# Contextual attention, two layers of four images on one core: feature buffers twice, sums ahead of arguments, exponentials behind copies

## What is computed

```python
raw_w = patches(b, 4, 2)                    # L = 1600 patches of 64 x 4 x 4
f = b[:, :, ::2, ::2]                       # 40 x 40
w = patches(f, 3, 1)                        # 1600 patches of 64 x 3 x 3
wn = w / maximum(norm(w), 1e-4)
yi = einsum('bpd,bld->blp', w, wn) * mm     # scores, 1600 x 1600
yi = softmax(yi * 10, axis=1) * mm
patches = einsum('blp,bld->bpd', yi, raw_w)
out = overlap_add(patches, stride 2)[pad:-pad] / 4
```

## Time and profile before

| | before |
|---|---|
| median of 3 runs | 1486.64 us (1485.1 to 1486.96) |
| the profiled execution, its own time | 1485.93 us |
| its span, first to last instruction | 1484.1 us |
| TensorE matmul, weight load busy | 1340.5 us (90%), 904.1 us (61%) |
| VectorE, ScalarE busy | 1195.3 us (81%), 853.7 us (58%) |
| GpSimd busy | 47.6 us |
| mean granted TensorE clock | 0.973 |

### The profile page before, as it was taken

One profiled execution on the slowest core, in us unless ns is written; L12 is line 12 of the kernel. 1 busy time (PEld: TensorE's weight loads), 2 busy tenths in 40 slices (PEclk: granted clock), 3 DMA queues, 4 the chain that ended last, 5 costly groups with the idle time before them and its releaser, 6 DMA issues.

```text
span 1484.1 us, 24228 instructions
## 1 busy us (share of the span) xinstructions
PE 1340.5 (90%) x7190; PEld 904.1 (61%) x7190; DVE 1195.3 (81%) x2830; ACT 853.7 (58%) x2233; POOL 47.6 (3%) x63
## 2 busy tenths in 40 slices
PE   4987999989999799998999899998999989999796
PEld 4765755667556675576656576566755666557343
DVE  4667889779888798878897878977888879888883
ACT  2667646656457564585555754666655755458431
POOL 1000000010000100001000000000000010000100
PEclk9997999999999999999999999999999999999999
DMA  5305462155622744137631556215462255412442
GB/s 101 45 1 133 108 130 70 51 150 116 127 61 65 172 101 109 52 85 165 122 93 34 130 128 136 78 44 143 119 124 72 62 143 113 111 51 83 129 137 57
DMA packets 181749, 146.57 MB, mean 99 GB/s; under 512 B 120114, under 2 KB 177522, under 8 KB 181618
## 3 DMA queue, kind: packets, MB, share of 16 engines
q1 hardware_dynamic: 181298, 144.04, 41.0%
q10 hardware_dynamic: 320, 0.99, 0.3%
HBM read 19.76 MB, written 13.11 MB: 22 GB/s over the span
## 4 chain that ended last, share of the span: by engine, by line
PE 32%; DVE 28%; SPq 11%; ACT 11%; issue 10%; DMA 7%; DVEq 0%; POOL 0%; ACTq 0%; POOLq 0%
PE psG L465 14%; PE psO L515 14%; DVE G L934 7%; DVE Z L967 5%; DVE G L874 4%; SPq L318 4%; DVE S L880 4%; DVE G L945 4%; ACT S L690 3%; ACT G L701 3%; SPq L299 3%; DMA HV<-LOHI 3%; PE psG L474 3%; ACT G L676 3%; DMA SH<-G 3%
## 5 line engine op out<-in xcount | busy, mean ns | idle before, releaser
L515 PE MATMUL psO<-Z,B 123*128 123x492 f32 (+2 forms) x1792 | 718.4, 530 | 38.5 <-DVE Z L967 25.2
L515 PEld LDWEIGHTS psO<-Z,B 123*128 123x128 f32 x1792 | 326.4, 194 | 238.1 <-issue 129.9
L465 PE MATMUL psG<-LH,HL 128*123 128x246 f16 (+2 forms) x2616 | 411.8, 287 | 38.2 <-DMA HV<-LOHI 28.7
L465 PEld LDWEIGHTS psG<-LH,HL 128*123 128x123 f16 x2616 | 280.5, 139 | 161.0 <-issue 96.7
L880 DVE CUSTOM_DVE_ANT_0 S<-G,RB 123x492 f32<-123x492 f32 (+1 forms) x448 | 269.1, 607 | 87.4 <-DVE G L874 55.0
L701 ACT ACTIVATE G<-G,nb 123x492 f32<-123x492 f32 (+1 forms) x448 | 267.0, 642 | 110.9 <-DVE G L934 110.4
L690 ACT ACTIVATE S<-S,nm 123x480 f32<-123x480 f32 (+3 forms) x560 | 307.3, 555 | 2.3 <-DVE nm L885 2.1
L945 DVE TENSOR_TENSOR G<-G,SH 123x492 f32<-123x492 f32 (+1 forms) x448 | 247.3, 591 | 54.2 <-DMA SH<-G 53.9
L934 DVE SCALAR_TENSOR_TENSOR G<-G,RA,psB 123x492 f32<-123x492 f32 (+1 forms) x448 | 270.1, 646 | 0.5 <-issue 0.5
L676 ACT ACTIVATE G<-psG 123x492 f32<-123x492 f32 (+3 forms) x256 | 120.1, 472 | 173.0 <-PE psG L465 92.5
L967 DVE TENSOR_TENSOR Z<-G 123x984 f32<-123x984 f32 (+2 forms) x192 | 197.3, 1028 | 0.6 <-PE psO L515 0.6
(11 more groups left out here) (83 smaller groups left out, 581.3 us busy)
## 6 DMA issues: line engine op xcount, KB each, us to landing
SH<-G SPq DMA_DIRECT2D x336, 214.8 KB
SH<-G SPq DMA_DIRECT2D x112, 89.2 KB
SH<-G SPq DMA_DIRECT2D x336, 19.2 KB
XP<-x SPq DMA_DIRECT2D x20, 280.0 KB, 5.9
XP<-mid SPq DMA_DIRECT2D x20, 280.0 KB, 5.3
HL<-LOHI SPq DMA_DIRECT2D x16, 246.5 KB, 3.5
mid<-OSB SPq DMA_DIRECT2D x48, 80.0 KB, 2.3
out<-OSB SPq DMA_DIRECT2D x48, 80.0 KB, 2.3
```

Source lines behind the costliest of these rows:

```text
L465: last = pe.matmul(psG[0:TW, bank, b0 * TW:b1 * TW], st[:, p:p + TW], mv[:, lo:lo + n], start=i == 0, stop=i == len(terms) - 1)
L515: last = pe.matmul(psO[:, b, 0:n], B[:, o:o + 128], Z[:, 2 * (s % 2) + j, 0:n], start=t == 0, stop=t == TILES - 1)
```

## The change

- `HL`, `LH`, `H1` and `HV` have two buffers each, taken in turn by the unit. ScalarE and VectorE write the high and low parts straight into the two halves of `LH`, so `LOHI` and the two DMAs for `LH` are gone: six DMAs (`N_F`) instead of eight.
- SyncE issues them in slots 10, 11 and 12 (one tile, two DMAs, each), behind the shifts and the strip of the slot, for unit w, instead of all in slot 28. They wait for the products of unit w - 2.
- VectorE: shifted sums and Z come first in every slot. The two arguments of the slot (now `argument_tile`) stand inside the score pair, after the add of the even tile and before its maximum; in slots without scores after Z; in slot 24 at the end, as before. `lse_sum` of slot 29 moves behind Z.
- The first Z of a chunk: its second half, which needs no strip, is made first, and only then comes the wait for the strip.
- ScalarE: the exponentials of the arguments stand behind both copies; in slot 24 the logarithm stands before the odd copy.
- TensorE: in slot 24 the row of logarithms is spread after the block group instead of before.
- Four memsets of the feature tiles and one of `LOHI` become one of `LH`.

```diff
-        HL = sb("HL", [128, FLEN], F16)   (and LH, H1, HV)
+        LH = sb("LH", [128, 2, FLEN], F16)   (and HL, H1, HV)
-        LOHI = sb("LOHI", [128, FLEN], F16)
-        LS, HS = LOHI[0:64, :], LOHI[64:128, :]
...
+        def halves_of(w):
+            return LH[0:64, w % 2, :], LH[64:128, w % 2, :]
...
             def lay_out_features(w, which):
+                if w >= 2:
+                    sp.wait_ge(g_ready, (w - 1) * NB)
+                    sp.sem_inc(sp_gate, 1)
...
-                    if s == SLOTS and w is not None:
-                        sp.wait_ge(g_ready, (v + 1) * NB)
-                        sp.sem_inc(sp_gate, 1)
-                        lay_out_features(w, ("HL", "LH", "H1", "HV"))
                     at = place(u, v, s + LEAD)
                     if at:
                         shift_pair(at)
                     at = place(u, v, s + 2)
                     if at and at[2] == 0:
                         shift_strip(at)
+                    if s in (10, 11, 12) and w is not None:
+                        lay_out_features(w, (("HL", "H1", "HV")[s - 10],))
...
-                    if s == 24 and v is not None:
-                        lse_row(v, w, 0)
...
                     if v is not None and 21 <= s < SLOTS - 1:
                         block_group(v, w, s - 21)
+                    if s == 24 and v is not None:
+                        lse_row(v, w, 0)
...
-            def high_features(v, w):
+            def high_features(w):
                 act.wait_ge(feat_in, (w + 1) * STRIPS * 16)
-                if v is not None:
+                if w >= 2:
                     act.sem_inc(act_gate, 1)
-                    act.wait_ge(f_in, (v + 1) * N_F * 16)
+                    act.wait_ge(g_ready, (w - 1) * NB)
...
                         copy_scores(u, v, j, 0)
+                        if s == 24:
+                            lse_log(v, False)
+                        copy_scores(u, v, j, 1)
                         if at and n == 0 and s != 24:
                             softmax_pair(at)
-                        copy_scores(u, v, j, 1)
                         if s == 23:
                             lse_exp(v, False)
-                        if s == 24:
-                            lse_log(v, False)
...
                         dve.tensor_tensor((odd if par else even)[:, b0 * TW:n], rows[:, p0 * TW:p0 * TW + n - b0 * TW],
                                           psG[0:TW, par, b0 * TW:n], ALU.add).then_inc(read, 1)
+                    if at and par == 0:
+                        argument_tile(at, 0)
+                        argument_tile(at, 1)
                     dve.wait_ge(s_read, v * NB + 2 * j + par + 1)
...
-                if i == 0:
-                    dve.wait_ge(shj_in, (u * NK + k + 1) * 16 * len(STRIP_PARTS))
-                    dve.sem_inc(dve_gate, 1)
...
-                    dve.tensor_tensor(Z[:, slot, 0:n], g[:, 0, c0:c0 + n], SHJ[:, 0:n], ALU.add)
-                    dve.tensor_tensor(Z[:, slot + 1, 0:n], g[:, 1, c0:c0 + n], g[:, 0, c0 - TW:c0 - TW + n],
-                                      ALU.add).then_inc(z_made, 1)
+                    dve.tensor_tensor(Z[:, slot + 1, 0:n], g[:, 1, c0:c0 + n], g[:, 0, c0 - TW:c0 - TW + n], ALU.add)
+                    dve.wait_ge(shj_in, (u * NK + k + 1) * 16 * len(STRIP_PARTS))
+                    dve.tensor_tensor(Z[:, slot, 0:n], g[:, 0, c0:c0 + n], SHJ[:, 0:n], ALU.add).then_inc(z_made, 1)
...
             def body(u, v, w):
                 for s in BODY:
                     at = place(u, v, s + LEAD)
-                    if at and s != 24:
-                        if s == SLOTS + 1:
-                            lse_sum(v, True)
-                        argument_pair(at)
                     at_y = place(u, v, s + AHEAD)
                     if at_y:
                         add_shifted(at_y)
...
                     if s == SLOTS + 1 and v is not None:
+                        lse_sum(v, True)
+                    pairs = score_list(s) if v is not None else []
+                    if at and not pairs:
+                        argument_tile(at, 0)
+                        argument_tile(at, 1)
+                    if s == SLOTS + 1 and v is not None:
                         lse_columns(v, True)
-                    if v is not None:
-                        for j in score_list(s):
-                            score_pair(v, j)
+                    for n, j in enumerate(pairs):
+                        score_pair(v, j, at if n == 0 and s != 24 else None)
...
-            pool.memset(LOHI[:, :].bitcast(F32), 0.0).then_inc(cleared, 1)
```

More of the change, by code:

```diff
@@ L244, in out_parts, with packs @@
                         yield a, j, at[0] - first, len(at), rows[at[0]] - 1 + a
-        def packs(which):
+        def halves_of(w):
+            return LH[0:64, w % 2, :], LH[64:128, w % 2, :]
+        def packs(w, which):
             n = FLEN
-            parts = {"HL": ((HL[0:64, :], HS), (HL[64:128, :], LS)), "LH": ((LH[0:64, :], LS), (LH[64:128, :], HS)),
-                     "H1": ((H1[0:64, :], HS), (H1[64:128, 0:n - 1], HS[:, 1:n])),
-                     "HV": ((HV[0:64, :], HS), (HV[64:128, 0:n - TW], HS[:, TW:n]))}
+            low, high = halves_of(w)
+            hl, h1, hv = (a[:, w % 2, :] for a in (HL, H1, HV))
+            parts = {"HL": ((hl[0:64, :], high), (hl[64:128, :], low)),
+                     "H1": ((h1[0:64, :], high), (h1[64:128, 0:n - 1], high[:, 1:n])),
+                     "HV": ((hv[0:64, :], high), (hv[64:128, 0:n - TW], high[:, TW:n]))}
             return [part for name in which for part in parts[name]]
@@ L297, in lay_out_features @@
                 sp.wait_ge(l_made, 2 * (w + 1))
-                for dst, src in packs(which):
+                for dst, src in packs(w, which):
                     sp.dma_start(dst, src).then_inc(f_in, 16)
@@ L457, in one_row, with products @@
                 return [(HL, LH, dy, dx) for dx in range(3)] + [(H1, H1, dy, 0), (HL, HL, dy, 2)]
-            def products(j, par, bank, b0, b1, terms):
+            def products(v, j, par, bank, b0, b1, terms):
                 s0 = S_CHUNKS[j // PAIRS][0]
@@ L488, in even_tile @@
                 if shared:
-                    last = products(j, 0, 0, stored, w, one_row(0))
+                    last = products(v, j, 0, 0, stored, w, one_row(0))
                 last.then_inc(g_ready, 1)
@@ L497, in odd_tile @@
                 if alone > stored:
-                    products(j, 1, 1, stored, alone, TERMS)
+                    products(v, j, 1, 1, stored, alone, TERMS)
                 if alone < w:
-                    last = products(j, 1, 1, alone, w, one_row(2))
+                    last = products(v, j, 1, 1, alone, w, one_row(2))
                 last.then_inc(g_ready, 1)
@@ L783, in _ @@
             act.wait_ge(l_made, 2)
-            for dst, src in packs(("LH", "HV")):
+            for dst, src in packs(0, ("HV",)):
                 act.dma_start(dst, src).then_inc(f_in, 16)
@@ L924, in lse_columns, with argument_tile @@
                 dve.tensor_tensor(lse[:, t], tot[:, t], big[:, t], ALU.max).then_inc(lse_dve, 1)
[L926 removed]
+            def argument_tile(at, j):
                 u, k, i = at
                 c0, n = p_cols(k)
[L929 removed]
+                t = arg_tiles(i)[j]
+                if i == 0 and j == 0:
                     dve.wait_ge(lse_rows, u * NK + k + 1)
                     dve.sem_inc(dve_gate, 1)
[L932 to L936 removed]
+                g = G[:, t * GLEN + c0:t * GLEN + c0 + n]
+                dve.scalar_tensor_tensor(out=g, in0=g, scalar=RA[:, bass.ds(u * TILES + t, 1)],
+                                         in1=psB[0:TW, k % 2, 0:n],
+                                         op0=ALU.mult, op1=ALU.subtract).then_inc(arg_made, 1)
             def add_shifted(at):
```

37 lines of the change are left out of this document (16 added, 21 removed).

## The result

The changed kernel takes 1552.96 us (median of 4 runs, 1551.22 to 1554.74) against 1486.8 us of the kernel before on the same chip: ratio 1.0446, 95% interval 1.0427 to 1.0464. Slower was forecast, but by 15 us and not by 66, and the time lies outside the range.

What follows compares the result with a forecast made beforehand. TensorE was taken as the limit in chunks 1 and 2, level with VectorE in chunk 0. 1485.9 + 11 (seven bodies) + 7 (last body) - 2 (ends) = 1502 us; range 1460 to 1522, the forecast's own 1489.5 to 1515.

Steps and rivals of the forecast that it cites:

- Features twice: At the boundary, TensorE's products no longer wait for feature copies: 3.1 to 5.0 us at each of 7, 22 to 35 us.
- Anchors (a) and (b): (a) slot 7's paste waits for ScalarE's read-out, moving 0.4 us; (b) slot 9's shift behind SyncE's stores and loads, 0.3 us.
- Strips: Z would wait for late strips: 2.2 us in slot 6, 1.5 in slot 13, 3.5 in slot 20, 1.8 in slot 27.
- In the bodies with scores this still fits: Arguments, exponentials and shift DMAs come 2.3 to 2.9 us later in the slot, but the shifts have two slots.
- rival 4: Shift DMAs become the bound in scored bodies too, when issue and landing exceed 5.5 us in chunk 0: 1558 us; chance 0.10.
- Bubble between add and maximum: VectorE's 0.19 us gap in the even tile is filled where VectorE sets the pace, chunk 0: 1 us per body.
- Copies at the new place: SyncE issues 5.4 us more in slots 10 to 12; it fits, cost 0 to 0.6 us per body, taken as 0.
- Where it gains again: Slots 21 to 27: sooner Z, logarithm ahead of the odd copy, row behind the block group give 1.5 us net per body.
- Last body: Without scores, the chain from sum to sum makes 3.95 us per slot instead of 3.53; with the strips, +7 us.
- TensorE busy 164 us within 1 per body: A sign: TensorE's busy time per body stays 164 us within 1, since the products' count and shapes are the same.
- Rival 2: TensorE makes its lags up, so only the boundary counts: 1469 us, or 1456 at 5.0 us per boundary; chance 0.07.
- Ends: First body gains 1.5 us in slots 24 to 28; the start saves 0.5 us from two small copies and three memsets.

Runs made afterwards that it cites:

- features kernel: Against the kernel before: only the feature buffers twice and six copies in slots 10 to 12, every order as before; 1446.72 us, ratio 0.9734.
- experiment 4: Against the changed kernel: arguments back ahead of both sums and exponentials back between the two copies; 1434.8 us, ratio 0.9656.
- experiment 10: Against the changed kernel: each tile shifted by one transfer of 122 partitions instead of two of 112 and 10; 2471.19 us, ratio 1.6612.

## Why the prediction was wrong

The step that failed is the delay of arguments, exponentials and shifts, taken as a fixed 2.3 to 2.9 us that "in the bodies with scores" still fits. With it the forecast came to +1.6 us a body and +7 us in the last one. Measured were +7.5 us a body (mean of six, 177.1 to 184.6) and +22.5 us at the end, and the arguments' place behind the two sums alone costs 134.4 us between otherwise equal kernels.

Sum of the medians, from before: 1486.7 - 40.0 (features) - 11.9 (small orders) + 48.4 (arguments behind the adds) + 86.1 (behind Z) - 14.6 (exponentials behind the copies) - 1.7 (arguments behind the even add) = 1553.0. Each term is a difference of neighbouring kernels above, in this order; in another order they would differ, since the moves interact (the exponentials' move alone is +26 on early arguments).

- **Features twice: right in kind, at the upper edge.** 22 to 35 us gross were forecast for seven boundaries. In the traces of before and of the features kernel the seven boundaries give 34.1 us of VectorE's time, 4.2 at the example and 4.8 to 5.2 at the others; the medians differ by 40.0. VectorE follows TensorE further than the 3.1 us of the lower edge. The example boundary had the shortest wait for the copies, 2.27 us of a mean of 4.1, and the clock behind the wait was in no term.
- **Anchors (a) and (b).** They were to move by 0.4 and 0.3 us and so swallow 4.6 of 5.0 us. In the features kernel nothing is swallowed: counted from the last minimum of the body before, the read-out of slot 7 comes 5.8 us sooner than before and the shifted sum of slot 11 4.9 us sooner (mean of six). In the changed kernel they move the other way, 1.0 and 4.5 us later, because the arguments come later. Behind the late read-out stand the pastes at a clock of 0.53, 2.7 us more a body, which no term has.
- **Strips: sizes right, price wrong.** Forecast stalls in slots 6, 13, 20 and 27: 2.2, 1.5, 3.5 and 1.8 us; measured 2.53, 1.59, 3.05 and 1.80. But only slots 13 and 20 were charged to TensorE; slot 6 was set against VectorE's lead and slot 27 against the gains. Without strips the kernel is 51.7 us faster.
- **"In the bodies with scores this still fits": the failed step.** The shifts were to fit within two slots. Their waits rose from 53.9 us (the row below, of before) to 95.1, and putting the arguments behind the adds alone costs 48.4. The forecast took the exponentials' delay as a fixed 2.3 to 2.9 us. It isn't fixed: once arguments queue behind a wait, each late transfer makes the next exponentials late, and with them the transfer after that, as the chain above goes from strip to argument to exponential. By the prediction's own sign, a slot of chunk 0 over 5.6 us with waits for shifts (slot 5: 7.25 us, with 2.93 us of waiting), that is rival 4, and its full price, 1558, is 5 us from the measured time. But rival 4's rule, issue and landing against twice the slot, names neither the arguments' queue nor Z, and it has nothing for the last body's 22.5 us: the close number is in part luck.

```profile
DVE G L945 <- DMA SH<-G: 53.9, 28, 5.1
```

- **Bubble between add and maximum.** Forecast 1 us a body; with the arguments right behind Z instead, the kernel is not slower beyond noise.
- **Copies at the new place:** 0 forecast; moved on to slots 16 to 18 the kernel changes by -1.2 us, with overlapping intervals. Right for this kernel.
- **Where it gains again:** slots 21 to 27 were to give 1.5 us a body net of the strip in slot 27. In the changed kernel VectorE's steps there give 1.6 us and slot 27 takes 1.1 back: 0.5 net. The small orders alone, on early arguments, give 1.7 (experiment 4).
- **Last body: +7 forecast, +22.5 measured, 20.4 of it by the order.** The chain from sum to sum was priced with the shift alone. Left out were the read-out behind the exponentials, the pastes behind the read-out, and the clock that falls after TensorE's idle time. Z follows Z by 3.5 to 3.9 us in quiet slots, as forecast (3.95), and by 7.0 in others.
- **TensorE busy 164 us within 1 per body:** the window above has 168.4, but also 913 matmuls against 897. From first product to first product (693.91 to 876.25) it is 166.2 us for 898, still outside. The clock, 0.97 against 0.99, stretches them; "busy" isn't work.
- **Rival 2** is refuted: it had 1456 to 1469 us, and the 11.6 us lost within a body are not made up in it. The share of weight loads on the page, 58%, leaves room by the Trainium skill's rule (Trainium Kernel Development and Optimization, Best Practices) quoted in the prediction; the time went to 1553 all the same.
- **Ends:** start -0.5 and first body -1.5 forecast, -2.2 and -4.6 measured. Of the 4.6 us 4.1 are the boundary's, which the forecast counts elsewhere, so 0.5 stands against its 1.5.

Only argued, not shown: how the 134 us behind the two sums divide between their waits, their own 1.2 us each and the clock that falls behind the late read-out; how the 86 us behind Z divide between strips and TensorE's buffers; and what a shorter issue alone would give.

## What to carry over

On an engine that works in order, put the instruction that feeds a long loop (here argument, exponential, transfer, sum) ahead of those that wait for its end. Here that place is worth 134 us of 1435. Behind them, every wait of one round is added to the next, and a forecast that moves each event by a fixed amount is far too small. An example row is only as good as its neighbours: a boundary taken from seven should be laid beside the six others first. When transfers are moved off one wait, look at where they now stand in the queue and what they bunch with: of the 4.5 us gained at slot 11, 3.4 stood again at slot 13 until the copies were moved on.

## What the runs showed of the hardware

- A shift of 122 partitions in one transfer takes 12.8 us in the chain of experiment 10, at a DMA share of 0.13 of the core's engines; as two of 112 and 10 the last one lands in 2.2 us. The low share means that the transfer of a whole tile was spread over few of the engines. The Trainium skill (DMA: Bandwidth & Descriptors, section Why a DMA increments its semaphore by 16 and not by 1) says that a transfer runs on the largest number of engines, up to 16, that divides the slowest dimension of both its ends: that is 2 for 122 partitions and 16 for 112. Two of sixteen are a share of 0.125, and the window's 0.13 agrees.
- Behind 5.4 us in which TensorE was idle the granted clock was 0.53 over the next 6.6 us, close to the lower level of 1.2 GHz, and a paste of 492 columns took 0.73 us, against 0.44 at a clock of 1.00 (eight in 3.54 us). So a stall of TensorE costs more than its own length: at a boundary of before 1.8 us on top of a wait of 4.16, at the read-out of slot 7 of the changed kernel 2.7 us a body; in the last body 234 matmuls took 98.7 us busy at a clock of 0.85 against 90.4 at 0.93 with arguments first.

```profile
1415.30:1550.30 135.00, 98.69 (x234) 49.79 (x234) 82.42 (x138) 36.17 (x75) 6.17 (x7) 0.85 0.33 92
```

```profile
1416.50:1530.80 114.30, 90.35 (x234) 45.35 (x234) 81.30 (x138) 36.48 (x75) 6.16 (x7) 0.93 0.39 108
```
